# A two-layer graph recommender on one core: GpSimd gathers every tile, where SyncE and ScalarE fetched one tile in 24 row by row

## The reference

```python
h = emb; acc = emb
for _ in range(2):                                  # LAYERS
    h = segment_sum(adj_val[:, None] * h[adj_col], adj_row, num_segments=N)   # 150,000 edges
    acc = acc + h
graph_item_embs = acc / 3
combined = graph_item_embs[items] + item_features[items]      # 512 sessions x 50 items
seq_hidden = take_along_axis(combined, alias_inputs[..., None], axis=1)
...                                                           # attention over each session
scores = (12 * l2norm(sess_emb)) @ l2norm(graph_item_embs).T  # 512 x 12,501
```

## Time and profile before

| | |
|---|---|
| median of 3 runs, no profile | 4178.22 us |
| the profiled execution's span | 6020.2 us |
| TensorE busy in the span (matmuls) | 3070.2 us, 51% |
| VectorE busy | 3014.4 us, 50% |
| GpSimd busy | 2890.1 us, 48% |
| ScalarE busy | 866.4 us, 14% |
| first gather of layer 0, last | 756.4, 3222.2 us |
| first gather of layer 1, last | 3262.6, 5555.2 us |

### The profile page before, as it was taken

How to read it: one execution, slowest core, us unless ns; L and a number is a source line. 1 busy time by engine, 2 the same in 40 slices (tenths; PEclk the granted TensorE clock), 3 DMA queues, 4 the chain that set the end, 5 groups by cost and what they waited for, 6 DMA issues and landing times.

```text
span 6020.2 us, 68764 instructions
## 1 busy us (share of the span) xinstructions
PE 3070.2 (51%) x9778; PEld 1849.5 (31%) x9778; DVE 3014.4 (50%) x7257; ACT 866.4 (14%) x3005; POOL 2890.1 (48%) x2965
## 2 busy tenths in 40 slices
PE   5988744444444444444444444444444444445578
PEld 3777622222222222222222222222222222222344
DVE  8999754444444444444444444444444444445455
ACT  2998800000000000000000000000000000000543
POOL 1666654444444444444445454454454454455561
PEclk8888866666666666666666666666666666666689
DMA  0000011111111111111114111111111111112454
GB/s 25 4 3 3 3 48 33 32 31 32 32 31 33 33 34 33 34 33 31 32 32 120 34 37 35 33 37 36 32 37 35 33 37 35 34 36 80 79 84 139
DMA packets 162229, 235.35 MB, mean 39 GB/s; under 512 B 67554, under 2 KB 107776, under 8 KB 161952
## 3 DMA queue, kind: packets, MB, share of 16 engines
q0 software_dynamic: 92896, 171.14, 12.4%
q1 hardware_dynamic: 54132, 58.90, 3.0%
q10 hardware_dynamic: 15052, 3.83, 0.3%
HBM read 192.69 MB, written 41.01 MB: 39 GB/s over the span
## 4 chain that ended last, share of the span: by engine, by line
ACTq 49%; issue 32%; DVE 7%; PE 6%; ACT 3%; another core or an unknown queue 2%; POOL 1%; DMA 0%; DVEq 0%; SPq 0%; POOLq 0%
ACTq L686 43%; ACTq L682 5%; ACT big L644 2%; PE bank L1520 1%; PE bank L1382 1%; POOL sorted_edges L542 1%; DVE stage L944 1%; PE bank L1548 1%; DVE acc L1167 1%; DVE big L888 1%; PE bank L1507 1%; DVE ring L896 0%; PE bank L1482 0%; DVE big L904 0%
## 5 line engine op out<-in xcount | busy, mean ns | idle before, releaser
L1444 PE MATMUL bank<-ring 128*128 128x256 f32 x4976 | 2105.7, 558 | 2135.8 <-DVE ring L1118 1194.1
L1444 PEld LDWEIGHTS bank<-ring 128*128 128x128 f32 x4976 | 1147.7, 263 | 3071.0 <-DVE ring L1118 1662.5
L574 POOL DMA_INDIRECT ring<-in_L_rec_emb,cring x1195 | 1134.9, 950 | 1336.2 <-ACT cring L662 978.9
L1167 DVE TENSOR_TENSOR acc<-acc,bank 128x256 f32 x2488 | 1029.6, 414 | 1481.3 <-remote 1131.6
L1118 DVE TENSOR_SCALAR ring<-bank,mlo,mval 128x256 f32<-128x256 f32 x2488 | 1343.5, 540 | 742.4 <-DMA ring<-in_L_rec_emb 523.1
L574 POOL DMA_INDIRECT ring<-table,cring x1195 | 1130.2, 946 | 1202.8 <-PE bank L1444 795.7
L644 ACT ACTIVATE big<-big 128x68 f32<-128x68 bf16 x1764 | 557.7, 405 | 1.2 <-issue 1.2
L1382 PE MATMUL bank<-big,ring 128*128 128x136 f32 x2352 | 430.8, 328 | 75.5 <-issue 20.8
L542 POOL DMA_INDIRECT sorted_edges<-moved,block_to x313 | 397.2, 1269 | 100.3 <-issue 100.0
L1382 PEld LDWEIGHTS bank<-big,ring 128*128 128x128 f32 x2352 | 356.8, 219 | 147.6 <-ACT big L644 83.2
L660 ACT COPY mlo<-ring 128x24 f32 (+1 forms) x104 | 21.7, 209 | 2415.0 <-issue 2381.6
(11 more groups left out here) (213 smaller groups left out, 1700.7 us busy)
## 6 DMA issues: line engine op xcount, KB each, us to landing
ring<-in_L_rec_emb SPq DMA_DIRECT2D x3136, 0.5 KB
ring<-in_L_rec_emb ACTq DMA_DIRECT2D x3136, 0.5 KB
ring<-table ACTq DMA_DIRECT2D x3136, 0.5 KB
ring<-table SPq DMA_DIRECT2D x3136, 0.5 KB
scores<-stage SPq DMA_DIRECT2D x48, 512.0 KB
ring<-in_L_rec_emb,cring POOLq DMA_INDIRECT x1195
ring<-table,cring POOLq DMA_INDIRECT x1195
table<-big SPq DMA_DIRECT2D x7, 896.0 KB, 9.1
```

The costliest lines, as they stand in the source:

```text
L574: pool.indirect_dma_start(msg[:, s, :], None, source, bass.IndirectOffsetOnAxis(cring[:, s:s + 1], 0)).then_inc(s_g[s], 16)
L1167: add = dve.tensor_tensor(acc[:, bass.ds(off, BUCKET)], acc[:, bass.ds(off, BUCKET)], bank[u % PR][:, 0:BUCKET], ALU.add)
L1444: pe.matmul(bank[u % PR][:, 0:BUCKET], msg[:, h * T + u, :], onehot[:, u % SR, :], start=True, stop=True).then_inc(s_mm[u % M], 1)
```

## The change

GpSimd gathers all 24 tiles of every stage, so 1244 in a layer. `own_rows`, `own_tiles`, `is_own`, the two DMAs L435, the three VectorE operations L1105 to L1107 and the semaphores `s_lines` and `s_line` are gone. The gather takes its indices straight from `m_col` and waits for `decode` (`s_mrdy`) in place of `fetch`; `cring` and its copy are gone. VectorE now waits for `fetch` (`s_mr`) before a stage's first one-hot. LEAD is 6 in place of 4, PR is 6 in place of 4. The transposed embeddings, which had banks 5 and 6, share bank 6, so TensorE's transposes of piece c wait for the add of piece c - 1.

```diff
-    SR, PR, LEAD = 8, 4, 4
+    SR, PR, LEAD = 8, 6, 6
...
-            def own_tiles(layer, source):
-
-                own_rows(source, 0, 1)
-                with sp.Fori(1, NST // 2 - 1) as i:
-                    for h in range(2):
-                        sp.wait_ge(s_mm[M - 1], i * (2 * T // M) + (PER * layer + T // M * (h - 1)))
-                        own_rows(source, i * (2 * HALF) + HALF * (h - 1), h)
-
-            sp.wait_ge(s_mrdy, 3)
-            own_tiles(0, emb_bytes)
...
             def gather_step(layer, source, c, h):
-                pool.wait_ge(s_mr, NST * layer + c + 1)
+                pool.wait_ge(s_mrdy, min(c, 1) + 1)
                 for u in range(tiles_of(c)):
                     s = h * T + u
-                    if is_own(T * c + u):
-                        continue
...
-                                            bass.IndirectOffsetOnAxis(cring[:, s:s + 1], 0)).then_inc(s_g[s], 16)
+                                            bass.IndirectOffsetOnAxis(m_col[:, T * c + u:T * c + u + 1], 0)
+                                            ).then_inc(s_g[s], 16)
...
-                act.copy(mval[:, h * T:(h + 1) * T], m_val[:, bass.ds(c * T, T)])
-                act.copy(cring[:, h * T:(h + 1) * T], m_col[:, bass.ds(c * T, T)]).then_inc(s_mr, 1)
+                act.copy(mval[:, h * T:(h + 1) * T], m_val[:, bass.ds(c * T, T)]).then_inc(s_mr, 1)
...
-            dve.wait_ge(s_lines, 32)
-            link(dve.tensor_copy(own_at.rearrange("o (k s) -> o k s", k=NOWN), own_lines[:, :, :, 0]))
-            link(dve.tensor_single_scalar(own_at, own_at, BUCKET.bit_length() - 1, ALU.arith_shift_right))
-            dve.tensor_single_scalar(own_at, own_at, LINE.bit_length() - 1, ALU.logical_shift_left).then_inc(s_mrdy, 1)
...
             def one_hot(layer, it, u):
 
-                if u % T < T - 1:
-                    dve.wait_ge(s_g[u], 16 * (FED[u] * layer + it + 1))
-                elif isinstance(it, int) and not is_own(2 * T * it + u):
-                    dve.wait_ge(s_g[u], 16 * (FED[u] * layer + (FED[u] if it else 1)))
-                else:
-                    dve.wait_ge(s_line[u // T], 16 * P)
-                    dve.sem_clear(s_line[u // T])
+                if u % T == 0:
+                    dve.wait_ge(s_mr, it * 2 + (NST * layer + u // T + 1))
+                dve.wait_ge(s_g[u], 16 * (FED[u] * layer + it + 1))
...
-                                  bank[5 + h][:, 0:2 * D], ALU.add).then_inc(s_ea, 1)
+                                  bank[6][:, 0:2 * D], ALU.add).then_inc(s_ea, 1)
...
                 pe.wait_ge(s_ec, c + 1)
-                pe.wait_ge(s_ea, c + 1)
+                pe.wait_ge(s_ea, c + 2)
```

More of the change, by code:

```diff
@@ L92, in recommender_program @@
     OPEN, NORMS = 5, 8
-    assert NST // 2 - 1 == L // 2 and HALF % AT_ONCE == 0 and NST % 2 == 0
-    assert NT <= N and NST % 2 == 0 and SG % Q == 0 and D == P and 0 < TAIL < P and T % SR == 0 and SR % PR == 0 and LEAD <= PR
+    assert NST // 2 - 1 == L // 2 and NST % 2 == 0
+    assert NT <= N and NST % 2 == 0 and SG % Q == 0 and D == P and 0 < TAIL < P and T % SR == 0 and T % PR == 0 and LEAD <= PR and LEAD <= SR - 2
     LOOP = 2 * min(NST // 2 - 1, L // 2, NB // 2)
@@ L103, in recommender_program @@
     TC = [T * (NST * n // 3) for n in range(4)]
-    HELD = "a column is held between 0 and N - 1, and an unused slot's is its tile's number, below NT <= N; a line has 512 bytes"
     FITS = "a tile's offset is 256 times the buckets that begin at or before it, less one: 0 to ROWS - 256"
-    def is_own(j):
-        return j % T == T - 1 and 1 <= j // T <= NOWN
-    FED = [sum(1 for j in range(u, NU, 2 * T) if not is_own(j)) for u in range(2 * T)]
+    FED = [len(range(u, NU, 2 * T)) for u in range(2 * T)]
     assert T % 4 == 0 and max(TC[n + 1] - TC[n] for n in range(3)) <= 512
@@ L230, in recommender_program @@
         block_at_l = carve(stage, NKL * P)
-        own_at = stage[0:2, 6 * D:6 * D + NOWN * HALF].bitcast(I32)
-        assert 6 * D + NOWN * HALF <= 4 * 512 * 2
         assert at[0] <= 4 * 512 * 2
@@ L244, in recommender_program @@
         mval = sb("mval", [P, 2 * T])
-        cring = sb("cring", [P, 2 * T], I32)
         startc = sb("startc", [P, 1])
@@ L340, in recommender_program @@
         s_iota = sem("s_iota")
-        s_lines = sem("s_lines")
-        s_line = [sem(f"s_line{h}") for h in range(2)]
         s_g = [sem(f"s_g{u}") for u in range(2 * T)]
@@ L397, in recommender_program @@
         s_out = [sem(f"s_out{i}") for i in range(4)]
-        emb_bytes = emb.rearrange("n d -> (n d)").bitcast(U8)
-        table1_bytes = table1.rearrange("n d -> (n d)").bitcast(U8)
-        msg_bytes = [msg[:, (h + 1) * T - 1, :].bitcast(U8) for h in range(2)]
         block = ctx.enter_context(nc.Block())
@@ L677, in _ @@
             fetch(0, 1, 1)
[L679 to L686, removed]
-                                      source[bass.ds(begin, LINE)].rearrange("(o b) -> o b", o=1)).then_inc(s_line[h], 16)
-            act.wait_ge(s_mrdy, 3)
-            own_rows(emb_bytes, 0, 1)
             with act.Fori(1, NST // 2 - 1) as i:
@@ L693, in _ @@
                     fetch(0, 2 * i + h, h)
-                    own_rows(emb_bytes, i * (2 * HALF) + HALF * (h - 1), h)
             for c in range(NST - 2, NST):
@@ L704, in _ @@
             act.wait_ge(s_t1w, 16 * (NB // GRP))
-            own_rows(table1_bytes, 0, 1)
             act.wait_ge(s_eld, 32)
@@ L716, in _ @@
                     fetch(1, 2 * i + h + 2, h)
-                    own_rows(table1_bytes, i * (2 * HALF) + HALF * (h + 1), h)
             for c in range(LOOP, max(NB, NST - 2)):
@@ L1435, in transpose_embeddings @@
                 pe.wait_ge(s_ec, c + 1)
-                pe.wait_ge(s_ea, c + 1)
+                pe.wait_ge(s_ea, c + 2)
                 for q in range(2):
-                    last = pe.transpose(bank[5 + h][:, q * D:(q + 1) * D], gnr[:, h, q, :], ident[:, :])
+                    last = pe.transpose(bank[6][:, q * D:(q + 1) * D], gnr[:, h, q, :], ident[:, :])
                 last.then_inc(s_eT, 1)
```

7 lines of the change are left out of this document (removed).

## The result

| | before | after |
|---|---|---|
| time without a profile, median | 4177.40 us (4175.29 to 4179.51, 4 runs) | 4296.41 us (4293.52 to 4298.50, 4 runs) |
| ratio | | 1.0286, 95% interval 1.0272 to 1.0301 |
| span of the profiled execution | 6020.2 us | 4292.8 us |

What follows compares the result with a forecast made beforehand. GpSimd's gather issue was taken to bound both layers. The terms 121.0 - 3.5 - 3.0 - 0.5 + 1.5 = +115.5 us, laid on the runs' median of 4178.2, gave 4294 us, +2.8%, range 4255 to 4312.

Steps and rivals of the forecast that it cites:

- The bound: Both layers: GpSimd's gather issue sets the stage, 28.8 us against 26 for ScalarE's rows and about 22 for VectorE; chance 0.80.
- 98 gathers at 1.235 us, +121.0: Stages 1 to 49 of both layers: one more GpSimd gather each, at 1.22 to 1.25 us, adds 121.0 us.
- Row DMAs at 0: ScalarE's and SyncE's queues: removing 12,544 row DMAs, their moves and 392 table reads saves 0, being hidden beside GpSimd's stage.
- VectorE's address operations, -3.5: Start of layer 0: without three 1.8 us operations, two gathers of 3.22 and 2.21 us return to 0.95, saving 3.5 us.
- The first products sooner, -3.0: Layer 0, tile 24: first products come 5.4 us sooner, so GpSimd's 3.30 us idle wait shrinks to the usual, saving 3.0 us.
- `m_col`, -0.5: Start of layer 0: the first gather no longer waits for three copies into cring, saving 0.5 us.
- LEAD 6, +1.5: Ends of both layers: six adds behind the last one-hot in place of four, about 0.8 us each time, 1.5 in all.
- The new waits, 0: Stage starts: VectorE's wait for fetch and TensorE's wait for the add of piece c - 1 cost 0.
- The stretched profile: First profile of before: recording instructions and gather packets stretched it 1842 us over the runs; after's span would be 4370 to 5900.
- The row queues as the bound: Rival, both layers: row DMA queues set the stage in the runs, so the change is faster, 4123 us at 1.15; chance 0.09.
- Hidden issue: Rival, both layers: gather issue is hidden or VectorE and TensorE set the stage; 98 gathers cost 0, 4173 us; chance 0.05.
- The rival with waits on top of the gathers: GpSimd also waits at its TensorE checks, say 3.3 us once in ten stages, 33 us more: 4327 us; chance 0.06.

Runs made afterwards that it cites:

- experiment 1: Kernel before with GpSimd gathering every tile and no row DMAs; addresses, cring, LEAD 4 and four banks stay: 4310.09 us, ratio 1.0289.
- Experiment 5: Kernel after with the last tile of stages 1 to 49 fetched by nobody, so no row DMAs and wrong sums: 4176.55 us, 0.9995 of before.
- experiment 9: Kernel before, unchanged, profiled a second time: span 4177.5 us, 4179.25 on record for that execution.
- Experiment 3: Kernel before with LEAD 6 and six banks, row DMAs kept: 4194.30 us, ratio 1.0009.
- experiment 8: Kernel before, row DMAs kept, with gathers indexed by m_col and the three address operations moved behind stage 0 of layer 0: 4177.90 us, ratio 0.9998.
- experiment 2: Kernel before with all gathers on GpSimd, no row DMAs, no own_lines loads and no VectorE address operations: 4311.06 us, ratio 1.0290.
- experiment 4: Kernel before with ScalarE fetching 96 rows of its own tile and SyncE 32, in place of 64 each: 5283.51 us, ratio 1.2611.
- experiment 7: Kernel after with one idle 128x256 VectorE operation added for each tile: 4298.49 us, 1.0288 of before.
- experiment 10: Kernel after with two idle 128x256 VectorE instructions added per tile: 5080.18 us, 1.2162 of before.

## Why the prediction was right, and where it was not

**The bound, right.** GpSimd's issue of gathers sets both layers in both kernels, against the chain and the waits of the profile that I had. Experiments 1 and 5 show it from both sides, and experiment 9 in the kernel before itself: steps of 1.25 us beside the row DMAs, ScalarE's rows done in 25.9 us of 28.8 (26 and 28.8 in the prediction). The room on ScalarE was smaller than the prediction had it, though: 1.5 us a stage by the estimate of experiment 9 and not 2.8, since the turn of its loop was left out. The prediction has the rows as the bound if they took 3 us more; by this estimate half of that is enough.

**98 gathers at 1.235 us, +121.0: a little small.** They cost 1.249, 122.4 us. The prediction lowered 1.251 because the parts outside the gathers summed to 1261.8 us. In the second profile of before they sum to 743.1 + 33.3 + 411.9 = 1188.3, and (4178.2 - 1188.3) / 2390 is 1.251: the first profile was stretched there too, and the row of the gather needed no correction.

**Row DMAs at 0: right.** Experiment 5 gives -2.6 us with all the other edits on top, in an interval of -5.9 to +1.7. The row DMAs are not without any effect: where they run, a gather lands 3.8 to 4.3 us after its issue at the median (experiments 3, 8 and 9), where it takes 2.5 without them (after, 1 and 5). GpSimd's steps are 1.25 us with both, so this delays no stage.

**VectorE's address operations, -3.5: right at their place.** Layer 0 has lost its steps of 2.53 and 3.63 us, some 4 us over 1.25 with the one behind them; experiment 2's layer 0 is 3.2 us shorter than experiment 1's. The Trainium skill, "SBUF — State Buffer", section "SBUF: two separate sides", cited in the prediction for this, agrees with the traces: the slow gathers come and go, and in experiment 8 move, with these operations. That it is the descriptors that are held back, no row shows. In the whole time of experiments 2 and 8 the saving can't be seen.

**The first products sooner, -3.0: wrong.** The wait of 3.30 us ahead of tile 24 was the stretched execution's. In the second profile of before the same gather, the 25th of the layer, comes without one:

```profile
777.44 0.94 POOL L574 DMA_INDIRECT ring<-in_L_rec_emb,cring  x1 [0.30 <-issue]
```

VectorE does reach its first one-hot 6.2 us sooner in after (752.90 against 759.05), but GpSimd was not waiting for it. I had read the long stalls of that profile as not real and this short one as real, with no reason to part them.

**`m_col`, -0.5: right** (743.1 to 742.7). **LEAD 6, +1.5: about right** where a row shows it: +0.7 to +1.2 between the layers (by pairs of profiles from one chip, and by after), and six adds at 3.17 us for four at 2.07. Experiment 3's +3.9 us has an interval that holds 1.5. **The new waits, 0: right.** GpSimd's 1.8 us for TensorE in the whole of after are six usual gaps.

Laid together from the two unstretched profiles: 122.4 for 98 gathers; the other steps of layer 0 -5.6 and of layer 1 -1.7; the start -0.4, between the layers +0.7, behind -0.1. That is +115.3 us, and so much do the spans differ. That the sum of the prediction was 115.5 is partly luck: a gather too cheap by 1.4 us in all, a saving of 3.0 that does not exist, and steps that are 0.001 us shorter over 2390 gathers, some 3.3 us, which the second profile of after (1.2500 and 1.2496) takes back. The interval of the median's 119.0, 113.6 to 125.7, holds both.

**The stretched profile: the conclusion right, the cause wrong.** The prediction took the 1842 us for the recording of instructions and of the gathers' packets, and gave 4370 to 5900 us for the span of after. It was 4292.8, with as many packets of gathers as ever; and the kernel before, recorded in full with 68,764 instructions both times, had a span of 4177.5 us the second time. The 1842 us belong to that one execution. What stalled it, no run here shows. What had saved the reading was that the span did not match the runs, and that register moves of 29 ns at the median took up to 1391 in it.

**Rivals.** The row queues as the bound fall with experiments 4 and 5: with half as many rows again on ScalarE they do set the stage, with 64 they do not. Hidden issue falls with the result: the rule quoted in the prediction from the Trainium skill, "DMA: Bandwidth & Descriptors", section "Issuing engines are not separate DMA queues", that issue time is usually small, does not hold for gathers of 128 single rows at 1.25 us each. In experiment 7 VectorE had 0.34 us a tile added and no time was lost, so VectorE does not set the stage. The rival with waits on top of the gathers falls too: no wait for TensorE longer than the usual gap is left in after.

## What to carry to other kernels

Compare the span of a profile with the time of the runs before reading any bound from it; where they differ, the medians of short instructions and the steps between neighbours in a quiet stretch can be used, single waits cannot, not even small ones, and a second profile is worth more than any correction. Work of two idle queues that takes 26 us beside an engine's 28.8 is free, and giving it to that engine costs its full price, however few the instructions. An engine's room is counted from start to start, over two stages if its loop holds two, and once it is used up, the small operations of its stage and the turn of its loop count as well (2.7 us on ScalarE in experiment 4, some 4.3 on VectorE in experiment 10).

## What the hardware showed that I had not expected

- VectorE's recorded lengths overlap. A 128x256 one-hot of 0.53 us, an add of 0.41 and a copy of 0.41 follow each other at 0.45, 0.33 and 0.34 us (experiment 7).
- One execution of a kernel can be 44% longer than its runs (6020.2 against 4178 us), with register moves of up to 1391 ns, when another profile of the same kernel has none over 29 (experiment 9).
- TensorE's granted clock differs between kernels whose products are the same, with no effect on the time. The same stretch of layer 0 in after and in experiment 7 (busy time by engine, clock, DMA share, GB/s):

```profile
1000.00:2200.00 1200.00, 940.34 (x1926) 442.16 (x1925) 853.03 (x2244) 12.95 (x80) 907.14 (x962) 0.65 0.20 53
```

```profile
1000.00:2200.00 1200.00, 786.34 (x1925) 338.22 (x1924) 1122.01 (x3207) 12.93 (x80) 906.85 (x962) 0.84 0.20 53
```

The same 962 gathers are made at 0.65 and at 0.84 of the full clock. In experiment 10, where TensorE waits longer for one-hots, the stretch has 0.50, which is the lower level (1.2 GHz) throughout; in the kernel before it has 0.72. What changes it between these kernels was not tried.
